# Selective-scan stage: on GpSimd the gate of a unit stands ahead of the product for the unit two later

## The reference, cut to what matters

```python
def step(h, inp):
    u_t, d_t, b_t, c_t = inp
    dA = jnp.exp(d_t[..., None] * A[None])
    h = dA * h + (d_t * u_t)[..., None] * b_t[:, :, None, :]
    y = jnp.einsum('bkdn,bkn->bkd', h, c_t)
    return (h, y)
```

## Time and profile before

| | us |
|---|---|
| median of 3 runs | 39340.68 (39318.74 to 39354.67) |
| the profiled execution | 39340.42 |
| its span, first to last instruction | 39338.6 |
| VectorE busy | 34763.5 (88%) |
| GpSimd busy | 33220.1 (84%) |
| TensorE busy | 27496.9 (70%) |
| ScalarE busy | 18062.4 (46%) |

### The profile page before, as it was taken

One profiled execution on the slowest core, in us unless ns is written; L12 is line 12 of the kernel. 1 busy time (PEld: TensorE's weight loads), 2 busy tenths in 40 slices (PEclk: granted clock), 3 DMA queues, 4 the chain that ended last, 5 costly groups with the idle time before them and its releaser, 6 DMA issues. The chain is left out here.

```text
span 39338.6 us, 330119 instructions
## 1 busy us (share of the span) xinstructions
PE 27496.9 (70%) x73952; PEld 7178.8 (18%) x73952; DVE 34763.5 (88%) x18992; ACT 18062.4 (46%) x22589; POOL 33220.1 (84%) x7824
## 2 busy tenths in 40 slices
PE   3777777777774777777777774777777777775777
PEld 1111111111111111111111111111111111111114
DVE  6999999999957999999999967999999999965994
ACT  2555555555522554554555522545455454523451
POOL 1999999999962999999999952999999999963994
PEclk6777777777766777777777766777777777777775
DMA  4666666666664666666666664666666666665665
GB/s 132 160 160 157 161 160 161 158 162 160 160 213 146 158 161 159 162 159 159 157 161 161 161 212 145 159 159 157 160 160 159 159 157 160 161 209 162 158 157 174
DMA packets 2388645, 6388.13 MB, mean 162 GB/s; under 512 B 692056, under 2 KB 835936, under 8 KB 2376032
## 3 DMA queue, kind: packets, MB, share of 16 engines
q1 hardware_dynamic: 2387040, 6374.58, 62.7%
HBM read 2973.68 MB, written 764.47 MB: 95 GB/s over the span
## 5 line engine op out<-in xcount | busy, mean ns | idle before, releaser
L1100 POOL TENSOR_TENSOR h<-h,c 128x2048 f32<-128x2048 f32 x4992 | 22509.1, 4525 | 1278.4 <-ACT state L959 1274.3
L901 DVE TENSOR_TENSOR_SCAN h<-decay,state,slot 128x1024 f32<-128x1024 f32 x6656 | 15615.9, 2346 | 681.1 <-ACT state L1047 20.1
L809 PE MATMUL psy<-h,t_fold 128*32 128x512 f32 x40000 | 12230.6, 787 | 265.6 <-ACT ybuf L1020 265.6
L744 PE MATMUL slot<-bc,pick 96*128 96x512 bf16 x13328 | 5060.7, 477 | 8763.4 <-DVE h L897 5512.5
L877 DVE TENSOR_TENSOR slot<-du,slot 128x1024 f32<-128x1024 f32 x6656 | 8050.7, 1210 | 1039.3 <-PE slot L744 945.0
L951 ACT ACTIVATE decay<-delta,na 128x1024 f32<-128x1024 f32 x6664 | 7583.2, 1146 | 2332.2 <-DVE h L901 2158.6
L897 DVE TENSOR_TENSOR_SCAN h<-slot,state,made 128x1024 f32<-128x1024 f32 x3328 | 7624.6, 2326 | 15.5 <-ACT slot L951 15.5
L1120 POOL TENSOR_TENSOR made<-du,b 128x2048 f32<-128x2048 f32 x1664 | 7524.6, 4522 | 127.1 <-DMA b<-bcdram 123.4
L951 ACT ACTIVATE slot<-delta,na 128x1024 f32<-128x1024 f32 x3328 | 3716.6, 1117 | 6481.4 <-DVE h L901 6476.4
L809 PEld LDWEIGHTS psy<-h,t_fold 128*32 128x32 f32 x40000 | 2244.1, 131 | 8523.9 <-issue 8231.2
L744 PEld LDWEIGHTS slot<-bc,pick 96*128 96x128 bf16 x13328 | 908.9, 104 | 14839.8 <-DVE h L897 8044.3
(11 more groups left out here) (103 smaller groups left out, 17260.9 us busy)
## 6 DMA issues: line engine op xcount, KB each, us to landing
delta<-delta SPq DMA_DIRECT2D x10048, 128.0 KB, 2.8
du<-du SPq DMA_DIRECT2D x10048, 128.0 KB, 2.9
c<-bcdram SPq DMA_DIRECT2D x6720, 128.0 KB, 2.8
b<-bcdram SPq DMA_DIRECT2D x6688, 128.0 KB, 3.0
u<-useq SPq DMA_DIRECT2D x212, 1536.0 KB, 6.6
yseq<-ybuf SPq DMA_DIRECT2D x624, 512.0 KB, 2.7
ya<-yseq SPq DMA_DIRECT2D x420, 512.0 KB, 4.3
yb<-yseq SPq DMA_DIRECT2D x360, 512.0 KB, 5.1
```

What stands on the lines that cost most here:

```text
L744: mm = pe.matmul(slot[s % 2][:, cols], pick[:, rows_of, :], bc[q % 2][:, cols], start=True, stop=True)
L809: mm = pe.matmul(psy[rows, cols], T["fold"][:, :], h[v % H_RING][:, c, cols], start=(v % QUADS == 0), stop=(v % QUADS == QUADS - 1), skip_ ...
L901: dve.tensor_tensor_scan(out, decay[s % DECAY_RING][:, order], slot[s % 2][:, order], first, ALU.mult, ALU.add).then_inc(sem["h_ready"], 1)
L1100: pool.tensor_tensor(both[:], both[:], c4[g][:].unsqueeze(1).broadcast_to((P, 2, CH)), ALU.mult)\
```

## The change

In GpSimd's loop the two calls in the body of the loop over units change places. Before, the product for unit v + 2 was issued ahead of the gate of unit v; now the gate of unit v is issued first. The number of instructions, their shapes and their semaphores stay the same. The rows of TensorE, VectorE, ScalarE and SyncE are the same in both kernels.

```diff
                     for v in range(BU):
                         if v % TILE_UNITS == DU_AT:
                             delta_u(i, v // TILE_UNITS + 1)
+                        gate(C0, i, v)
                         if v + POOL_LEAD in on_pool:
                             multiply(i, v + POOL_LEAD)
-                        gate(C0, i, v)
```

## The result

The changed kernel takes 42768.71 us (median of 4 runs, 42760.24 to 42773.17), against 39329.71 us of the kernel before on the same chip: a ratio of 1.087, with a 95% interval of 1.0857 to 1.0884. The forecast was 42460 us, in a range of 42000 to 43200. So it is slower by 3439 us, where 3120 were forecast.

The account below looks back on a forecast made before the run. VectorE's work bound the kernel; the new loop was to replace it: 8 x 21.07 + 2.26 + 1.8 = 172.6 us a chunk against 157.6, 15.0 x 208 = 3120 us more, giving 42460 us, range 42000 to 43200.

Parts of the forecast that it names:

- What bounds: Before the change VectorE's own work fills 153.6 of 157.6 us a chunk; it never waits for GpSimd's product.
- The loop: Scan, save, gate, product, scan: every triple's third unit waits about 2.3 us; a triple takes 21.07 us against 18.78.
- What the window swallows: VectorE's longer wait hides one of three corrections and nearly all slot stalls, 4.0 us a chunk; two corrections add 2.26.
- Unit 12: Once a chunk du, waiting for delta, stands directly ahead of this unit's gate and delays it: 1.8 us a chunk.
- X: Start of VectorE's second scan of U0, the first unit of a triple; the loop's steps are timed from it.
- X + 2.57: End of ScalarE's save of a triple's first unit, 2.57 us after its second scan starts; the gate follows by 0.08.
- GpSimd is free by then: When the first unit's save ends, GpSimd has finished three earlier gates, so the gate can start at once.
- The clock: TensorE's clock may fall with more idle time, lengthening the delta chain to unit 12: 2 us a chunk, 400 us.
- rival A: TensorE's clock falls, slot stalls partly stay, unit 12's chain lengthens: 2 to 4 us a chunk more, 43200 us; chance 0.17.
- B: Faster: earlier gates bring earlier folds and fills, slot is filled in time, product still ready; 38510 us; chance 0.02.
- C: No effect: the product begins while the gate waits, or the save comes early enough; 39340 us; chance 0.02.
- D: Hand-overs overlap, so the loop is shorter: 20.7 us a triple, 42000 us or a little less; chance 0.11.

Follow-up runs that it names:

- The split product: Changed kernel with the product for each triple's third unit made in two instructions, one per scan step, each scan waiting for its own; 40193.36 us, ratio 1.0206.
- the longer lead: Changed kernel, gate still first, but the product issued three units ahead instead of two; 39378.39 us, ratio 0.9997.

## Why the prediction was right, and what was off

- **What bounds.** Right: before, VectorE never waited for the product; now it does 1662 times.
- **The loop.** Right, link by link: 21.07 us forecast and measured. The split product took it away again, and so did the longer lead.
- **What the window swallows.** Right in kind: the correction of unit 10 costs nothing. The other two cost 1.15 and 0.94 us a chunk instead of 1.13 each. Stalls on `slot` fell from 945.0 to 520.7 us, not to the few layer starts: the prediction had called its size wrong above 500.
- **Unit 12.** 1.8 us forecast, 1.62 measured. But the reason was half of it: I named du ahead of the gate, and the save is late there too (X + 3.15 in the mean, and X + 3.29 already before). Removing du alone gained 0.1 us, so the right number was in part luck.
- **The mis-sized term.** The step that failed is the save at "X + 2.57" (that is its end; it starts at X + 2.38), taken from one triple and used for all eight; the sum has nothing for a late save at unit 9. "GpSimd is free by then" held there: it idled 4.38 us in front of the gate. The save started at X + 4.15 instead, and that triple took 22.83 us instead of 21.07: 1.76 x 208 = 366 us. Units 12 and 18 came out 0.18 and 0.19 us shorter than forecast, the others 0.17 longer together, which leaves 1.56 a chunk, 324 us, for the 319 between forecast and measurement. The trace of before could have told: its save of unit 9 starts at X + 3.21 in the mean. With that lateness alone the term would have been (3.21 - 2.38) x 208 = 173 us, an estimate; the rest goes with the lower clock, which after the change is there in every chunk.
- **The clock.** The prediction had it among the bounds and in rival A, up to 2 us a chunk at unit 12. There it wasn't lower than before (0.81 in the mean against 0.73, over the stretch named above); it was lower at unit 9 (0.50 against 0.70, from 2.4 to 8 us after the scan of unit 8). So A was true in part, at another place and inside the range.
- **B, C and D** fell. The kernel is slower, not faster or the same; each of the 1664 products starts 4.46 to 4.52 us after the gate of its own U0 starts, never ahead of it; and the ordinary triple took 21.07 us, not 20.7.

## What to carry to other kernels

When an engine's queue gets a wait in front of work that another engine needs, follow the wait back. If it leads to that same engine, there is now a loop, and its period, the sum of all its links, replaces the busy time of the busiest engine. Here an idle time of 3.9 us between product and use was spent, and 2.3 us a triple owed, by the exchange of two calls. Then look at every place where the new link is served by a queue with other work in it, and write down its slack at each, over many turns and not over one: at unit 9 one chunk of before showed 0.27 us of slack, and in half of all chunks the save was late by 0.9 us or more. An engine that idles more may also run slower when it is next needed, as TensorE did here at unit 9.

## What the runs showed of the hardware

In all 208 chunks of the changed kernel TensorE had idled for 5.1 to 5.6 us in front of the fill behind unit 8's first scan, and its granted clock was at the lower level through the work behind; fills and pairs of matmuls took 1.03 and 2.07 us instead of 0.60 and 1.12. In the kernel before the clock was as low there in 75 chunks, after 3.1 to 3.2 us of idle time, and mostly at the upper level (0.8 or more in the mean) in 100, after 0.2 to 1.8 us. Idle time was not needed for a fall: with 32-row matmuls in the gap it fell while they ran, and stood at 0.50 over the fill; with as many 128-row matmuls it was at 1.00 over the fill and fell about 3 us later. Added work that nobody used made the kernel 501 us faster.

The Trainium skill (TensorE: Matmul & The Clock Gate, Part 1: The HAM clock gate) says that the throttled clock is the default and that activity releases it. The trace agrees in part: the chunks with the longer idle time (3.1 us and more) are those with the lower clock, but the fall under the 32-row matmuls came with TensorE at work, which that sentence alone does not tell.
